# k computed by tokens in seven products of quarters, with its turns, banks and loads moved to match

## The chip, the cores and the metric

One core of one Trainium2 chip runs the kernel. The metric is the device time of one execution in microseconds (us). The kernel before took 1389.52 us, the median of three runs (1387.83 to 1391.02).

## The reference, cut to what matters

x has 4 sequences of 1024 tokens with 1024 channels. Every token is normalised, and two branches use it: an attention with a decaying state, and a gated ffn. All three weight matrices are rounded to -1, 0, 1 times one scale.

```python
x = L0_attn_x
xn = _layernorm(x, axis=-1)
s = _L0_attn_ref(xn, ...)
g = _silu(_L0_ffn_ref(xn, L0_ffn_weight, L0_ffn_bias))
x = x + s * g
```

Inside the attention (16 heads of 64, chunks of 128 tokens, a state S from chunk to chunk within a sequence):

```python
h = _rmsnorm(x, qkv_norm_w, eps)
qkv = h @ _weight_quant(qkv_w).T
scores = jnp.einsum('bhtd,bhsd,hts->bhts', qi, ki, mask)
intra = jnp.einsum('bhts,bhsd->bhtd', scores, vi)
cross = jnp.einsum('bhtd,ht,bhde->bhte', qi, lam_t, S)
o = scale * (intra + cross)
kv = jnp.einsum('bhtd,ht,bhte->bhde', ki, lam_rev, vi)
S = lam_T * S + kv
out = _rmsnorm(_rmsnorm(out, norm_w, 1e-06), proj_norm_w, eps) @ _weight_quant(proj_w).T
```

## The kernel before, in words

The 4096 tokens are handled as 16 blocks i of two chunks c of 128 tokens. Chunk number g = 2i + c; every eighth chunk ends a sequence, so blocks 3, 7, 11 and 15 hold a chunk that passes no state on. Everything is one program per engine with the order written out by hand, and semaphores between them (`s_...`). Activations are split into two 16-bit parts, high and low, each multiplied by fp8 weights, so every product is made twice and added in PSUM.

**Banks.** PSUM has four banks `ring`, used in the fixed order of the list `ring_uses`: use n may begin when use n-4 was emptied (`free_bank`, `emptied`). Four more banks, `att_ps`, hold scores, outputs and the state's update.

**A block on TensorE (PE), i from 2 on.** `project_qk(i, j)`, j = 0 to 7, makes q (j < 4) and k (j >= 4) by channels: 32 matmuls of 256 columns for each j. Between them stand, for the chunk before, `output_scale` (the sum of squares over channels, two tiny matmuls), `spread_gamma` (its inverse root, spread over partitions) and the two halves of `project_out`. Then v by tokens: where a full product of two chunks by 1024 channels takes eight products of quarters, v takes seven (p1 to p7, 8 matmuls of 512 columns each), with sums of quarters of the activations (`sum_b`, S1 to S4) and of the weights (`sum_v_weights`, T1 to T4) made on VectorE and GpSimd. ffn is made the same way (`sum_y`, `sum_weights`, `product`). Several products share a bank: `add_v`, `begin_v` and the `take_...` functions read it between two of them, so the later product waits for that reading. Then `attention(i, 0)` and `attention(i, 1)`: scores, k turned to tokens (`turn_k`, 8 transposes), outputs, state's update, `project_out` of chunk 0.

**VectorE (DVE).** At a block's start: statistics of block i+1 (`norm_stats`), sums of quarters and low parts (`sum_y`, `low_part`), `output_scale` (the small steps before the inverse root), `scale_o`, `split_o`, `sum_b`, `gate_out` of the chunk before, `low_b_sum`, then `centre` (two operations over 128x1024 for each chunk, which normalise x as turned by the host), then the second `gate_out`.

**ScalarE (ACT)** makes the high parts, empties q and k banks (`qk_out`) and applies silu. **GpSimd (POOL)** sums the squares (`sum_squares`), adds into the output (`add_out`), makes the inverse roots (`norm_scale`, `output_scale`), decays q and the state, and makes the sums of weights once, in block 1. **SyncE (SP)** issues all DMAs of the loop from one queue: store, mean and deviation of each token out to memory and back to all partitions (`spread_norm`), turned x (`load_turned`, which waits until block i's sums have been read out of `y` and `y_odd`), and x.

Of the kernel before, what the change touches and what calls it, by code (L numbers as in the profile page):

```python
# [36 lines left out]
def program(nc, x, qkv_w, proj_w, decay, ffn_w, ffn_b, norm_cols, x_turned, out):  # L37
# [17 lines left out]
    with ExitStack() as ctx:  # L55
# [49 lines left out]
        norm_rows = sb("norm_rows", [P, T, CHUNKS, 2])  # L105
# [6 lines left out]
        x_third = sb("x_third", [P, C])  # L112
        assert ARENA + SQ + C + C + C + C + CHUNKS * 2 * T + SUMS + CHUNKS * C == RAW * C
        gate_odd = sb("gate_odd", [P, CHUNKS, C])
        q_t = arena[:, Q_OFF:K_OFF].rearrange("p (r t) -> p r t", r=PR)
# [27 lines left out]
        ln = sb("ln", [P, 4, 24])  # L143
        og = sb("og", [P, 2, 4])
# [6 lines left out]
        norm_out = nc.dram_tensor("norm_out", [T, CHUNKS, 2], F32).ap()  # L151
# [34 lines left out]
        s_x = [sem(f"x_loaded{k}") for k in range(6)]  # L186
        s_out = [sem(f"out_stored{k}") for k in range(6)]
# [8 lines left out]
        s_vseed, s_vbase, s_vsum = sem("v_bank_begun"), sem("v_base_made"), sem("v_sum_made")  # L196
        s_zpart, s_zbase, s_zbias = sem("z_part_made"), sem("z_base_made"), sem("z_base_biased")
# [20 lines left out]
        def x_slot(i, c):  # L218
            if c == 1:
                return 2 + i % 3  # L220
            return i % 2 if i < 4 else (5, 0, 1)[(i - 4) % 3]

        def x_tile(i, c):
            k = x_slot(i, c)
            return xt[:, k, :] if k < 4 else x_third[:, :] if k == 4 else gate_odd[:, 0, :]

        def x_turn(i, c):

            return sum(x_slot(k, c) == x_slot(i, c) for k in range(i))
# [49 lines left out]
        def of_product(i, name):  # L279
            return 2 * CHUNKS * HALF + len(PRODUCTS) * (i - 2) + PRODUCTS.index(name) + 1  # L280

# [6 lines left out]
        def of_z(i, c, h):  # L288

            return of_ffn(i, c, h) if i < 2 else CHUNKS * HALF * i + ((0, 0), (1, 0), (1, 1), (0, 1)).index((c, h)) + 1  # L290
# [13 lines left out]
        def of_pair(i, c):  # L304
            return CHUNKS * (i - 2) + c + 1

# [20 lines left out]
        def v_weights_of(name):  # L327
# [5 lines left out]
            return qkv_q[:, k * CPH:(k + 1) * CPH, 2 * C + n * BANK:2 * C + (n + 1) * BANK]  # L333

# [85 lines left out]
        for i in range(NB):  # L420
# [13 lines left out]
            for c in range(CHUNKS):  # L434
                last = is_last(chunk(i, c))
# [8 lines left out]
                if not last:  # L444
                    ring_uses += [("k", i, c, 0), ("k", i, c, 1)]
# [5 lines left out]
                else:  # L451
# [4 lines left out]
                    for h in range(HALF):  # L456
                        ring_uses.append(("proj", i, 0, h))
                        if i == NB - 1:
                            ring_uses.append(("spread" if h else "total", NB - 1, 1))
        ring_uses += [("proj", NB - 1, 1, h) for h in range(HALF + 1)]  # L460
        ring_n = {use: n for n, use in enumerate(ring_uses)}

# [9 lines left out]
        def emptied(use):  # L472
# [8 lines left out]
            if kind == "ffn":  # L481
                return s_z, of_ffn(*use[1:])
            if kind == "v product":
# [7 lines left out]
            if kind == "v":  # L491
                return s_v, of_half(*use[1:])
            if kind == "k":
                return s_kl, HALF * passes_on(chunk(use[1], use[2])) + use[3] + 1
# [41 lines left out]
        def tensor_program(pe):  # L536
# [61 lines left out]
            def product(i, name):  # L598
# [8 lines left out]
                else:  # L607
# [3 lines left out]
                    if name == "p3":  # L611
                        pe.wait_ge(s_z, of_z(i, 1, 1))
                    else:
                        pe.wait_ge(s_zpart, of_zpart(i, ("p2", "p7", "p4").index(name)))
# [32 lines left out]

            def project_qk(i, j):
# [246 lines left out]
        def vector_program(dve):  # L895
# [381 lines left out]
            def attention(i, c):  # L1277
# [14 lines left out]
                if not last:  # L1292
                    decay_k(i, c)
# [799 lines left out]
```

## Time and profile before

| what | us |
|---|---|
| median of 3 runs | 1389.52 |
| the profiled execution | 1388.52 |
| its span, first to last instruction | 1386.8 |
| PE busy | 1344.0 |
| DVE busy | 950.2 |
| POOL busy | 603.6 |
| ACT busy | 552.1 |

The span is what the profile shows; 1.7 us of the execution lie around it. Matmuls are pipelined: one is shown for longer than the time from its start to the next one's start, so the cost of a row of them is read from starts. The granted TensorE clock is 0.995 on average over the span.

### The profile page before, as it was taken

The page shows a single profiled execution, that of the slowest core. Times are in us where ns is not written, and L with a number is a line of the kernel's source. Part 1 is how long each engine was busy: PE and PEld are TensorE (multiplying, and loading weights), DVE is VectorE, ACT ScalarE, POOL GpSimd, SP SyncE. Part 2 cuts the span into 40 slices and gives each one's busy share as a digit, 9 for nine tenths or more (in the row PEclk, how much of TensorE's full clock was granted, in tenths as well). Part 3 has the DMA queues.
Part 4 walks back from the last instruction along what each step waited for, and adds up shares of the span by engine and source line. Part 5 has one row for each costly group of instructions (what it writes and reads, how often), then busy time and mean ns, then how long its engine had stood idle before and what let it go on. Part 6 is the DMA issues. An engine that isn't in the chain of part 4 may idle for free.

```text
span 1386.8 us, 27408 instructions
## 1 busy us (share of the span) xinstructions
PE 1344.0 (97%) x11313; PEld 935.1 (67%) x11313; DVE 950.2 (69%) x1463; ACT 552.1 (40%) x1074; POOL 603.6 (44%) x528
## 2 busy tenths in 40 slices
PE   5999989899999999999999999999999999999998
PEld 2577667576676767767666676767767676776765
DVE  7895648486685857758576784858668585775835
ACT  5893224343343434334343423534334343433421
POOL 1533775263353525445351445426335352544332
PEclk9999989999999999999999999999999999999999
DMA  9521101103020020202002020110302002020000
GB/s 363 214 92 57 29 31 62 54 4 97 1 70 31 32 69 1 85 16 69 32 30 71 1 69 32 36 65 2 100 1 69 32 32 69 2 69 1 17 16 32
DMA packets 25534, 74.69 MB, mean 54 GB/s; under 512 B 6465, under 2 KB 6721, under 8 KB 25410
## 3 DMA queue, kind: packets, MB, share of 16 engines
q1 hardware_dynamic: 25120, 72.92, 15.5%
q8 instruction: 90, 1.47, 0.4%
q14 instruction: 34, 0.28, 0.1%
q10 hardware_dynamic: 290, 0.02, 0.0%
HBM read 56.12 MB, written 16.81 MB: 53 GB/s over the span
## 4 chain that ended last, share of the span: by engine, by line
PE 68%; POOL 14%; DVE 10%; issue 4%; ACT 2%; DMA 2%; SPq 0%; DVEq 0%; POOLq 0%; ACTq 0%
PE ring L658 20%; PE ring L617 12%; PE ring L643 12%; PE ring L777 8%; PE att_ps L693 4%; POOL sq L1855 4%; DVE b_lo L1097 4%; PE att_ps L739 2%; POOL xt L1876 2%; PE att_ps L735 2%; POOL sq L1851 2%; PE ring L701 2%; DVE o_lo L1243 1%; PE att_ps L716 1%; POOL diag L1870 1%
## 5 line engine op out<-in xcount | busy, mean ns | idle before, releaser
L658 PE MATMUL ring<-b_lo,qkv_q 128*128 128x256 f16 x2048 | 451.2, 273 | 0.0
L658 PE MATMUL ring<-b_hi,qkv_q 128*128 128x256 f16 x2048 | 451.2, 273 | 0.0
L658 PEld LDWEIGHTS ring<-b_hi,qkv_q 128*128 128x128 fp8e4 x2048 | 201.6, 98 | 27.8
L658 PEld LDWEIGHTS ring<-b_lo,qkv_q 128*128 128x128 fp8e4 x2048 | 200.3, 98 | 28.0
L777 PE MATMUL ring<-proj_q,o_hi 128*128 128x512 fp8e4 x496 | 188.1, 379 | 2.9 <-DVE o_lo L1243 2.9
L777 PE MATMUL ring<-proj_q,o_lo 128*128 128x512 fp8e4 x496 | 188.0, 379 | 0.0
L1599 ACT ACTIVATE arena<-ring,wscale 128x512 f32<-128x512 f32 x64 | 44.0, 687 | 213.0 <-PE ring L658 213.0
L1851 POOL TENSOR_TENSOR sq<-sq,cols 128x1024 f32<-128x1024 f32 x29 | 55.0, 1896 | 160.7 <-DVE b_lo L1097 152.3
L1876 POOL TENSOR_TENSOR xt<-xt,gate_even 128x512 f32<-128x512 f32 x40 | 59.9, 1507 | 147.4 <-DVE gate_even L1263 147.3
L1081 DVE SCALAR_TENSOR_TENSOR arena<-ring,wscale,arena 128x512 f32<-128x512 f32 x28 | 21.0, 750 | 139.2 <-PE ring L643 139.2
L1855 POOL TENSOR_TENSOR sq<-sq 128x1024 f32<-128x1024 f32 (+1 forms) x58 | 109.6, 1890 | 4.5
L1592 ACT ACTIVATE arena<-ring,wscale 128x512 f32<-128x512 f32 x64 | 43.9, 686 | 157.1 <-PE ring L658 157.1
L1128 DVE SCALAR_TENSOR_TENSOR gate_even<-ring,ln,gate_even 128x512 f32<-128x512 f32 x70 | 52.4, 749 | 68.5 <-PE ring L617 68.5
L739 PE MATMUL att_ps<-arena 128*64 128x128 f32 x1024 | 95.4, 274 | 0.0
L1811 POOL TENSOR_TENSOR gate_even<-gate_even,bias 128x512 f32<-128x512 f32 x14 | 17.7, 1264 | 167.1 <-ACT gate_even L1552 167.1
L735 PE MATMUL att_ps<-arena 128*64 128x128 f32 x896 | 89.1, 278 | 0.0
L777 PEld LDWEIGHTS ring<-proj_q,o_hi 128*128 128x128 f16 x496 | 48.6, 98 | 57.9 <-DVE o_lo L1243 4.0
L1181 DVE TENSOR_TENSOR arena<-att_ps,mask 128x512 f32<-128x512 f32 x128 | 79.5, 682 | 9.8 <-PE att_ps L693 9.8
L1826 POOL TENSOR_TENSOR arena<-arena,lam_q 128x512 f32<-128x512 f32 x56 | 71.3, 1285 | 32.4 <-PE att_ps L739 32.3
L777 PEld LDWEIGHTS ring<-proj_q,o_lo 128*128 128x128 f16 x496 | 48.6, 98 | 53.2
L1576 ACT ACTIVATE gate_even<-gate_even 128x512 f32<-128x512 f32 x60 | 37.3, 625 | 115.2 <-DVE gate_even L1128 115.2
L693 PEld LDWEIGHTS att_ps<-arena 64*128 64x128 f32 x1024 | 59.7, 188 | 17.7 <-issue 13.8
(222 smaller groups left out, 2864.0 us busy)
## 6 DMA issues: line engine op xcount, KB each, us to landing
raw<-in_qkv_w SPq DMA_DIRECT2D x24, 512.0 KB, 15.8
xt<-in_x SPq DMA_DIRECT2D x23, 512.0 KB, 3.5
out<-xt SPq DMA_DIRECT2D x22, 512.0 KB, 2.6
y<-in_x_turned SPq DMA_DIRECT2D x14, 512.0 KB, 6.1
y_odd<-in_x_turned SPq DMA_DIRECT2D x14, 512.0 KB, 6.8
raw<-in_ffn_w SPq DMA_DIRECT2D x8, 512.0 KB, 9.7
norm_rows<-norm_out SPq DMA_DIRECT2D x14, 256.0 KB, 5.2
raw<-in_proj_w SPq DMA_DIRECT2D x6, 512.0 KB, 4.5
```

The lines of the kernel that those rows point to most:

```text
L617: ins = pe.matmul(ring[:, b, :], of[:, j, :], weights_of(weights)[:, j, :], start=(begins and j == 0 and k == 0), stop=(j == CPH - 1 and k ...
L643: ins = pe.matmul(ring[:, b, :], of[:, j, :], v_weights_of(weights)[:, j, :], start=(name in ("p1", "p5") and j == 0 and k == 0), stop=(j ...
L658: ins = pe.matmul(ring[:, b, e * BT:(e + 1) * BT], qkv_q[:, cb, o:o + P], part[:, cb, :], start=(cb == 0 and part is b_hi), stop=(cb == NC ...
L693: ins = pe.matmul(att_ps[:, 2 * half + e, j, :], k_t[rows, r, ts], q_t[rows, r, ts], start=True, stop=True)
L735: pe.matmul(att_ps[e * D:(e + 1) * D, half, j, :], state[:, passes_on(g) % 2, r, e * D:(e + 1) * D], q_decay[:, r, :], start=True, stop=Fa ...
L739: ins = pe.matmul(att_ps[e * D:(e + 1) * D, half, j, :], v_tok[:, c, r * P + e * D:r * P + (e + 1) * D], scores_m[:, half, e, j, :], start ...
L777: ins = pe.matmul(ring[:, b, :], part[:, cb, :], proj_q[:, cb, cs], start=(cb == 0 and k == 0), stop=(cb == NCB - 1 and k == 1))
L1181: dve.tensor_tensor(scores_m[:, half, e, :, :], att_ps[:, 2 * half + e, :, :], mask[:, e, half * CPH:(half + 1) * CPH, :], ALU.mult).then_ ...
L1826: pool.tensor_tensor(q_decay[:, hs, :], q_t[:, hs, c * T:(c + 1) * T], lam_q[:, hs, :], ALU.mult).then_inc(s_ql, 1)
L1851: pool.tensor_tensor(sq[:, 1, :, :], sq[:, 0, :, :], over_tokens(cols[:, 1, :], T), ALU.mult).then_inc(s_sqw, 1)
L1855: pool.tensor_tensor(sq[:, :, 0:m, :], sq[:, :, 0:m, :], sq[:, :, m:2 * m, :], ALU.add).then_inc(s_sqw, 1)
L1876: pool.tensor_tensor(o, o, gate_of(i)[:, c, cs], ALU.add).then_inc(s_add, 1)
```

## The change

1. **k by tokens (from block 3, `BY_TOKENS`).** `project_qk` runs for j = 0 to 3 alone. `k_product` makes k as v is made: seven products, with the `sum_b` parts that v uses anyway, and sums of k's weights by `sum_k_weights` on POOL (T1 and T2 in block 2, T4 and T3 in block 3). The result is k by tokens (`k_tok`, in the memory of `gate_odd`); `turn_k` now turns it the other way, to channels, for every chunk, the last of a sequence too. ACT copies the turned k (`turned_k`); DVE decays k by tokens in place (`decay_k_tokens`) instead of from PSUM (`decay_k`).
2. **Orders from block 3 on** on PE, DVE and ACT are new: `attention_by_tokens`, and the block's start. On DVE the four `sum_b` now stand between the two `norm_stats`, ahead of `output_scale`, and `low_part` of the four sums after the first `gate_out`, right ahead of `centre(i + 1, 0)`.
3. **ffn's products** run p1, p6, p2, p5, p7, p3, p4 (before: p1, p6, p2, p7, p4, p5, p3).
4. **Totals and spreads** from chunk (2, 1) on stand in `att_ps` bank 3 (`aside`) instead of `ring`.
5. **x is loaded twice**: `load_x` into `xt[0:2]` for the statistics, `load_x_out` into `xt[2:4]` for the sum with the output. `norm_stats` of blocks 2 and 3 move to the start of blocks 1 and 2.
6. **`norm_rows`** has tokens innermost; the store of mean and deviation writes single fp32 elements.
7. **POOL in block 1**: `sum_v_weights` after `decay_state` and `decay_q`, not ahead of them.

```diff
-        norm_rows = sb("norm_rows", [P, T, CHUNKS, 2])
+        norm_rows = sb("norm_rows", [P, CHUNKS, 2, T])
...
+        BY_TOKENS = 3
+        PRODUCTS_LATER = ("p1", "p6", "p2", "p5", "p7", "p3", "p4")
...
+            def k_product(i, name):
+
+                if (i, name) == (BY_TOKENS, "p1"):
+                    pe.wait_ge(s_kwsum, 4)
...
+                elif name == "p4":
+                    pe.wait_ge(s_ksum, of_k_pair(i, 1))
...
+            def attention_by_tokens(i, c):
+                last = is_last(chunk(i, c))
+                scores(i, c)
+                if c == 0:
+                    v_product(i, "p4")
+                    product(i, "p1")
+                    product(i, "p6")
+                    turn_k(i, 1)
+                else:
+                    product(i, "p5")
+                    product(i, "p7")
+                    output_scale(i, 0)
+                    product(i, "p3")
+                    product(i, "p4")
+                    spread_gamma(i, 0)
+                outputs(i, c, 0)
+                outputs(i, c, 1)
+                if not last:
+                    update_state(i, c)
+                if c == 0:
+                    product(i, "p2")
...
+            for i in range(BY_TOKENS, NB):
+                project_qk(i, 0)
+                project_qk(i, 1)
+                output_scale(i - 1, 1)
+                project_qk(i, 2)
+                spread_gamma(i - 1, 1)
+                project_qk(i, 3)
+                k_product(i, "p1")
+                project_out(i - 1, 1, 0)
+                k_product(i, "p5")
+                k_product(i, "p2")
+                k_product(i, "p6")
+                project_out(i - 1, 1, 1)
+                k_product(i, "p3")
+                k_product(i, "p7")
+                k_product(i, "p4")
+                v_product(i, "p1")
...
+            def add_k(i, c):
+
+                dve.wait_ge(s_kps, of_k_product(i, "p7" if c else "p3"))
...
+                if more:
+                    norm_stats(i + 1, 0)
+                for name in Y_SUMS:
+                    sum_b(i, name)
+                if more:
+                    norm_stats(i + 1, 1)
+                output_scale(i - 1, 1)
...
+                gate_out(i - 1, 1, 0)
+                for name in Y_SUMS:
+                    low_part(i, name)
+                if more:
+                    centre(i + 1, 0)
+                gate_out(i - 1, 1, 1)
+                add_k(i, 0)
+                add_k(i, 1)
...
+                if i + 2 < NB:
+                    load_x(i + 2, 0)
+                    load_x(i + 2, 1)
+                if 2 < i + 1 < NB:
                     for c in range(CHUNKS):
                         load_turned(i + 1, c)
```

How the orders move, at three places. `ring` is the four shared banks, `arena` the memory of q, k, v, sums and state, `y` and `y_odd` the turned x of chunk 0 and 1.

PE in the changed kernel, block 5, from k's seventh product in program order to v's first (p7's last matmul, p4, v's p1):

```order
L731 MATMUL ring<-qkv_q,b_sum_lo 128x512
L731 MATMUL ring<-k_sum_last,b_hi 128x512 [waits k_sum_made]
L731 MATMUL ring<-k_sum_last,b_lo 128x512
...
L705 MATMUL ring<-qkv_q,b_hi 128x512 [waits k_tokens_made]
L705 MATMUL ring<-qkv_q,b_lo 128x512
```

Nothing stands between k's p7 and p4, and p4 waits for `k_sum_made`, DVE's `add_k(i, 1)`, which reads p7's bank. In the kernel before k had no such pair; v's p7 and p4 have a product of ffn between them (before) or the scores (now).

DVE at a block's start, before (block 10):

```order
L1263 SCALAR_TENSOR_TENSOR gate_even<-ring,wscale,gate_even 128x512 [waits gate_made,proj_ps] x2
L985 BN_STATS ln<-gate_odd 128x6 [waits x_loaded5]
...
L1044 TENSOR_TENSOR a_lo<-y_odd,a_hi 128x4x128 [waits a_hi_made]
L1060 TENSOR_TENSOR y_odd<-y_odd 128x512 [waits a_lo_made,b_weighed,b_lo_made]
L1060 TENSOR_TENSOR y_odd<-y,y_odd 128x512 [waits a_lo_made,y_summed]
L985 BN_STATS ln<-xt 128x6 [waits x_loaded3]
```

and in the changed kernel, from the same `gate_out` on:

```order
L1441 SCALAR_TENSOR_TENSOR gate_even<-ring,wscale,gate_even 128x512 [waits gate_made,proj_ps] x2
L1133 BN_STATS ln<-xt 128x6 [waits x_loaded0]
...
L1216 TENSOR_TENSOR arena<-arena 128x512 [waits b_summed,b_weighed] x4
L1133 BN_STATS ln<-xt 128x6 [waits x_loaded1]
...
L1428 TENSOR_SCALAR og<-att_ps 128x1 [waits sq_total_ps]
```

One low part and two sums of y stood between the statistics; now it is the four sums of b (`sum_b`), then the same second statistics and the small steps on `og`.

POOL in the changed kernel, at block 3's start, after the two norm scales:

```order
L2095 TENSOR_TENSOR ln<-ln,wscale 128x1 [waits ln_amp]
L2129 TENSOR_TENSOR k_sum_last<-qkv_q,k_sum 128x2048 [waits k_weights_summed]
L2129 TENSOR_TENSOR qkv_q<-qkv_q 128x4x512 [waits k_weights_summed,qk_ps]
L2202 TENSOR_TENSOR xt<-xt,gate_even 128x512 [waits gated,x_loaded_for_out1] x2
```

The two sums of k's weights (T4, T3) are new there; PE's first k product waits for both.

## Rows read from the trace of the kernel before

**Rows 1.** The page's part 1: busy us (share), instructions of each engine.
```profile
PE 1344.0 (97%) x11313; PEld 935.1 (67%) x11313; DVE 950.2 (69%) x1463; ACT 552.1 (40%) x1074; POOL 603.6 (44%) x528
```

**Rows 2.** Waits of PE: who waited for whom: us in total, times, longest us.
```profile
PE ring L643 <- ACT ring L1533: 3.8, 1, 3.8
PE att_ps L693 <- DVE arena L1216: 3.7, 1, 3.7
PE ring L670 <- DVE gate_even L1263: 2.9, 1, 2.9
```

**Rows 3.** Windows after two of these waits: busy by engine, PEclk, DMA share, GB/s.
```profile
174.60:178.00 3.40, 3.35 (x8) 1.19 (x9) 2.39 (x4) 0.00 (x0) 3.33 (x3) 0.51 0.36 147
257.10:262.00 4.90, 4.82 (x17) 1.95 (x18) 0.00 (x0) 1.31 (x3) 4.82 (x5) 0.72 0.40 127
```

**Rows 4.** Timeline of PE, block 8: first and last of 64 q matmuls, of 40 v matmuls.
```profile
714.92 0.27 PE L658 MATMUL ring<-b_hi,qkv_q 128*128 128x256 f16 x1
...
721.80 0.27 PE L658 MATMUL ring<-b_lo,qkv_q 128*128 128x256 f16 x1
...
750.68 0.38 PE L643 MATMUL ring<-qkv_q,b_hi 128*128 128x512 fp8e4 x1
...
759.10 0.38 PE L643 MATMUL ring<-qkv_q,b_sum_lo 128*128 128x512 fp8e4 x1
```

**Rows 5.** Timeline of PE, block 8: eight transposes of k, and what follows.
```profile
768.32 1.04 PE L701 MATMUL ring<-ident,arena 128*128 128x128 f32 x8
769.28 0.44 PE L739 MATMUL att_ps<-arena 128*64 128x128 f32 x4
```

**Rows 6.** Timelines of PE and DVE, block 7: a bank handed over and back.
```profile
700.36 0.38 PE L617 MATMUL ring<-ffn_sum,sum_lo 128*128 128x512 fp8e4 x1
...
701.67 0.38 PE L617 MATMUL ring<-ffn_q,sum_hi 128*128 128x512 fp8e4 x1 [0.60 <-DVE gate_even L1128]
```
```profile
700.77 0.75 DVE L1128 SCALAR_TENSOR_TENSOR gate_even<-ring,ln,gate_even 128x512 f32<-128x512 f32 x1 [0.98 <-PE ring L617]
```

**Rows 7.** Timeline of DVE, start of block 9, between and behind the statistics.
```profile
799.00 0.68 DVE L1044 TENSOR_TENSOR a_lo<-y_odd,a_hi 128x512 f16<-128x512 f32 x1
799.81 1.54 DVE L1060 TENSOR_TENSOR y_odd<-y_odd 128x512 f32<-128x512 f32 x1
801.38 1.10 DVE L1060 TENSOR_TENSOR y_odd<-y,y_odd 128x512 f32<-128x512 f32 x1
...
804.96 0.16 DVE L1252 SCALAR_TENSOR_TENSOR og<-og,ring 128x1 f32<-128x1 f32 x1
```

**Rows 8.** Timelines of POOL and PE, start of block 9.
```profile
801.90 2.94 POOL L1876 TENSOR_TENSOR xt<-xt,gate_even 128x512 f32<-128x512 f32 x2
805.20 0.94 POOL L1866 TENSOR_TENSOR og<-og,halves 128x1 f32<-128x1 f32 x1 [0.36 <-DVE og L1252]
```
```profile
807.35 0.49 PE L765 MATMUL ring<-diag,mean_sq 128*128 128x128 f32 x2 [0.42 <-POOL diag L1870]
```

**Rows 9.** Groups by line and form, DVE: busy us, mean ns of one | idle before.
```profile
L1068 DVE TENSOR_TENSOR arena<-arena 128x512 f32<-128x512 f32 x56 | 38.6, 690 | 4.7 <-DVE arena L1068 0.5
L1236 DVE TENSOR_TENSOR ow<-ow,ring 128x1024 f32<-128x1024 f32 x31 | 37.9, 1221 | 26.0 <-PE ring L765 25.9
```

**Rows 10.** The page's part 6, DMA issues: count, KB each, median us to landing.
```profile
xt<-in_x SPq DMA_DIRECT2D x23, 512.0 KB, 3.5
...
y<-in_x_turned SPq DMA_DIRECT2D x14, 512.0 KB, 6.1
```

**Rows 11.** Timelines of POOL and PE, block 8: squares summed, PE's total.
```profile
778.82 0.73 POOL L1860 TENSOR_TENSOR sq_sum<-sq 128x256 f32<-128x256 f32 x1
```
```profile
781.12 0.50 PE L757 MATMUL ring<-mean_w,sq_sum 128*128 128x1 f32 x4
```

**Rows 12.** POOL: a sum of weights (groups), block 3's last norm scale (timeline); PE, block 3's q.
```profile
L1804 POOL TENSOR_TENSOR v_sum_last<-qkv_q,v_sum 128x2048 fp8e4<-128x2048 fp8e4 x1 | 3.8, 3822 | 0.1
```
```profile
318.13 0.19 POOL L1782 TENSOR_TENSOR ln<-ln,wscale 128x1 f32<-128x1 f32 x1
```
```profile
302.04 0.27 PE L658 MATMUL ring<-b_hi,qkv_q 128*128 128x256 f16 x1
```

More of the change, by code:

```diff
@@ L216, in chunk, with x_new, x_out, mean_of @@
             return i * CHUNKS + c
[L218 to L229, printed above, removed]
+        def x_new(i, c):
+            if i == 0:
+                return xt[:, CHUNKS + c, :], (s_xo[c], DMA)
+            return xt[:, c, :], (s_x[c], DMA * i)
+        def x_out(c):
+            return xt[:, CHUNKS + c, :]
+        def mean_of(i, c, n=1):
+            return norm_pair[:, i % 2, c, 0:n]
+        def deviation_of(i, c):
+            return norm_pair[:, i % 2, c, 1:2]
         def gate_of(i):
@@ L419, in program @@
         ring_uses += [("v", 0, 0, 0), ("mean", PROJ), ("v", 0, 0, 1)]
-        for i in range(NB):
+        for i in range(BY_TOKENS):
             if i > 0:
@@ L745, in output_scale @@
             def output_scale(i, c):
-                b = free_bank("total", i, c)
+                if aside(i, c):
+                    pe.wait_ge(s_scm, 2 * HALF * (chunk(i, 1) + 1))
+                else:
+                    free_bank("total", i, c)
+                to = total_of(i, c)
                 if summed_at_once(chunk(i, c)):
@@ L763, in spread_gamma @@
                 pe.wait_ge(s_gamma, chunk(i, c) + 1)
-                b = bank_of("spread", i, c) if one_bank(i, c) else free_bank("spread", i, c)
-                pe.matmul(ring[:, b, 0:T], mean_sq[:, :], diag[:, c, :], start=True, stop=True).then_inc(s_spread, 1)
+                if aside(i, c):
+                    pe.wait_ge(s_os, chunk(i, c))
+                elif not one_bank(i, c):
+                    free_bank("spread", i, c)
+                pe.matmul(spread_of(i, c), mean_sq[:, :], diag[:, c, :], start=True, stop=True).then_inc(s_spread, 1)
             def project_out(i, c, half):
@@ L839, in attention @@
                     project_out(i, 0, 0)
-                    if not more:
-                        output_scale(i, 1)
                     project_out(i, 0, 1)
@@ L869, in tensor_program @@
             project_v(0, 0, 1)
-            for i in range(NB):
+            for i in range(BY_TOKENS):
                 if i > 0:
@@ L1011, in centre @@
                 to = y_turned[c]
-                rows = [norm_rows[:, :, c, k].unsqueeze(1).to_broadcast([P, NCB, T]) for k in range(2)]
+                rows = [norm_rows[:, c, k, :].unsqueeze(1).to_broadcast([P, NCB, T]) for k in range(2)]
                 dve.wait_ge(s_xt[c], DMA * n)
@@ L1247, in output_scale @@
                 k = og[:, c, :]
-                bank = ring[:, bank_of("total", i, c), :]
+                bank = total_of(i, c)
                 dve.wait_ge(s_sqt, g + 1)
@@ L1291, in attention @@
                     output_scale(i, 0)
-                if not last:
-                    decay_k(i, c)
+                decay_k(i, c)
                 if (i, c) == (0, 0):
@@ L1301, in attention @@
                         take_b(1, 1, 0)
-                    elif more:
+                    else:
                         split_b(i + 1, 0, 0)
@@ L1310, in attention @@
                 weight_o(i, c, 1)
-                if not last:
-                    add_state(i, c)
+                add_state(i, c)
                 if c == 0:
@@ L1323, in attention @@
                 else:
-                    if more and i > 0:
+                    if i > 0:
                         split_b(i + 1, 0, 1)
@@ L1398, in vector_program @@
                 round_weights(key)
-            for i in range(NB):
-                if 2 < i < NB - 1:
+            for i in range(BY_TOKENS):
+                if i > 0:
                     norm_stats(i + 1, 0)
@@ L1720, in scalar_program @@
                 weights_out(kind, t)
-            for i in range(NB):
+            for i in range(BY_TOKENS):
                 if i > 1:
@@ L2045, in sync_program @@
             for c in range(CHUNKS):
-                for i in range(NB - 3, NB):
-                    last = len(LAST_COLUMNS) - 1 if (i, c) == (NB - 1, 1) else 0
-                    sync.wait_ge(s_out[x_slot(i, c)], DMA * (x_turn(i, c) + 1 + last))
+                sync.wait_ge(s_out[c], DMA * (NB + c * (len(LAST_COLUMNS) - 1)))
         tensor_program(nc.tensor)
```

419 lines of the change are left out of this document (325 added, 94 removed).

## The prediction, written before the changed kernel was run

> **What bounds the kernel now.** I began with the page's busy times: PE is busy 1344.0 of 1386.8 us, DVE 950.2, POOL 603.6 [rows 1]. Nothing else is near, so only two things can move the time: work on PE, and waits of PE. The list of PE's waits came next. Its three longest behind the first 100 us are single ones, in blocks 1 and 2, of 3.8, 3.7 and 2.9 us [rows 2]; the rest come once in a block and are below 1 us. Third, the windows behind such waits: PE's granted clock is 0.51 over 3.4 us after one and 0.72 over 4.9 us after another [rows 3]. That is the lower level, 1.2 of 2.4 GHz, for some 3.3 and 2.7 us, so each of these waits costs about 1.5 us more than it shows. Last, I read PE's, DVE's and POOL's timelines of one block beside each other, since an order this tight has no slack that an average would show.
>
> A measurement of this kernel can tell about 0.2% (2.8 us) from no change; faster and slower mean more than that here.
>
> **The sum.** It is made against the profiled execution, 1388.5 us, which is 1.0 us under the median of the runs. 13 blocks (3 to 15) change; 12 of them (3 to 14) also prepare a next block.
>
> *k's products.* 64 q matmuls of 256 columns start 6.88 us apart, first to last: 6.88/63 = 0.109 us each. 40 of 512 columns take 8.42/39 = 0.216 each [rows 4]. k was 128 x 0.109 = 13.98 us and becomes 56 x 0.216 = 12.10: 1.88 less a block, **-24.5 us** in 13. All of it is on PE's path.
>
> *Turning.* k was turned for 28 chunks, and not for those that end a sequence; now for all 32. Eight transposes take 0.96 us [rows 5]: **+3.9** for four.
>
> *The new wait at k's p4.* p4 follows p7 on the same bank, and DVE's `add_k(i, 1)` must read between them. The kernel before had such a handover in ffn in the four blocks that end a sequence: the last matmul starts at 700.36, DVE reads from 700.77 for 0.75 us, PE goes on at 701.67 [rows 6]. That is 1.31 us where 0.216 would do: 1.1 us lost with nothing between. Thirteen times: **+14.2**. On PE all of v's products and both chunks of the block are queued behind it. It is 1.1 only if DVE is free. DVE's chain, from the end of `project_out(i-1, 1, 0)`, is `gate_out` 0.75, four low parts of 0.68 [rows 7], turned x of chunk 0, which SP may only issue then, `centre` (two operations that I take at 1.22, the price of a contiguous 128x1024 operation [rows 9]), `gate_out`, `add_k` twice, 0.75 each, and some 0.4 of handovers. With the load at 3.5 us, as x lands, this makes 12.0; with 6.1, as turned x lands behind other transfers [rows 10], 14.6. PE has 56 matmuls over the same time, 12.1, plus the 1.1 of the handover: 13.2. So 0 to 1.4 us come on top; two loads of x now stand ahead in SP's queue, which speaks for the late end, but were issued some us earlier. I take 0.4 in 12 blocks: **+4.8**.
>
> *The spread of the chunk before.* PE has waited for it: DVE's small steps end at 805.12, POOL starts 0.1 later, PE goes on at 807.35 [rows 7, 8]. In between is nothing but the chain, so whatever DVE has more ahead of the small steps goes through to PE. One low part and two sums of y leave (0.68, 1.54 and 1.10 [rows 7]), four sums of b come. Alone they take 0.69 each [rows 9]: by bare durations the difference is 2.76 - 2.06 = +0.7. But the sum of y that took 1.54 ran while POOL worked on squares, and POOL's two adds end only at 804.84 [rows 8]: at 1.5 each the four take 6.0, +2.7. I take 1.2, nearer the lower end, because of the three operations in that stretch one was not stretched at all: 12 x 1.2 = **+14.4**.
>
> *ffn's order.* With p7 now between p5 and p3, and p3 between p7 and p4, DVE has 1.7 us or more for each handover. The 0.77 that PE lost in four blocks (1.1 less 0.36 of the total's matmuls) goes: **-3.1**. But p7 left the stretch ahead of the total: PE reaches it 8 x 0.216 = 1.73 earlier, at 779.39 where it was 781.12, and POOL's squares end at 779.55 [rows 11]. That is 0.2 us of waiting in 13 blocks: **+2.6** (0 to 0.6 each).
>
> *Blocks 1 and 2.* Statistics earlier, POOL's sums of v's weights later, and a `gate_out` between the two `centre` take away what all three waits of [rows 2] hang on: 3.05 + 3.83 + 3.93 from start to start, and 1.5 us of low clock after each: **-15.4**. I saw no work that would take their place.
>
> *k's weights.* PE's first k product waits for four sums of weights. T1 and T2 fit into POOL's idle time of block 2. T4 and T3 stand behind the norm scales of block 3, which end at 318.32; two sums of 3.8 end at 326.0. Block 3 begins at 302.04 and PE reaches k after q (13.98), the total and the spread (0.7) and its wait (1.6), at 318.3 [rows 12]. **+7.7**, and 1.5 of low clock after such a wait: **+9.2** (7 to 12).
>
> *At nothing:* totals and spreads in `att_ps` (the bank's readers are done 1 us before); x twice (the loads are 3.5 us [rows 10] and not needed for tens of us); the store in single elements (turned x is later still); ACT's five more emptyings a block, 0.69 each (it is busy 40% of the time [rows 1]). If ACT were late, PE would wait for the k bank's seed at k's p2, where there is 0.1 us of room.
>
> Sum: -24.5 + 3.9 + 14.2 + 4.8 + 14.4 - 3.1 + 2.6 - 15.4 + 9.2 = **+6.1**: 1394.6 for the profiled execution, 1395.6 as a median. Its own range, with the ends of k's p4, the spread, the total and the weights that can come together, is 1382 to 1416.
>
> **The rule weighed.** The stretched sums of y [rows 7] show that DVE and POOL can hold each other up. The Trainium skill (SBUF — State Buffer, "SBUF: two separate sides") says more: a DVE instruction with two SBUF inputs and a POOL instruction exclude each other for the whole of an instruction. By that rule each of the four sums of b could wait out one POOL instruction, and the spread would cost the upper end. It is the third rival below.
>
> **The rivals.**
> 1. *The waits are covered: faster.* If DVE's start of the block is no slower than before, turned x lands in time and squares are ready, the terms of 4.8, 14.4 and 2.6 are nothing: 1388.5 - 15.7 = 1373, 1374 as a median. For it: DVE is idle 31% of the time [rows 1], and the terms that rest on PE's rows alone already sum to -15.7. Against it: DVE is on PE's path exactly at the two places where work is put in. It decides at 1.2 us in a block: if these three terms come to less than that in sum, the change is faster; more, slower.
> 2. *Low clock after the new waits: slower.* Waits of 3 to 4 us were followed by 1.2 GHz [rows 3], waits of 1.1 us [rows 6] were not. If the waits at k's p4 and at the spread, of 1 to 2.5 us each, are long enough in most blocks, 1.5 us come on top in 12: +18, 1414.
> 3. *DVE and POOL in turns: slower.* The spread at +2.7 in a block instead of 1.2: +18, 1414.
> 4. *Blocks 1 and 2 don't gain*, because another chain is right behind (the loads of x for block 2, POOL's ffn weights): +15, 1411.
>
> **How the numbers follow.** The sum as it stands 0.43, rival 1 0.30, rivals 2 and 3 0.11 each, rival 4 0.05. The predicted time is the likeliest case's, 1395.6. The range takes in rival 1 and the slow ones: 1372 to 1418. Faster by over 0.2%: rival 1, and 0.04 from the lower end of the likeliest: 0.34. Within 0.2%: 0.12, all from the likeliest. Slower: 0.54.
>
> **What would show it.** Right: blocks whose PE time without waits is 1.9 us shorter; a wait of PE in front of the last k weights product for DVE, 13 times, 0.9 us or more; a wait in front of the spread for POOL that grew from 0.4 to over 1 us; one wait of 7 us or more in block 3 for POOL's weights; none over 1.2 us in blocks 1 and 2. Wrong: DVE's small steps no later after a block's first q matmul than before, turned x landed before the low parts end, or a granted clock below 1.00 in the later blocks. If the longest waits of a block are for ACT, I looked at the wrong engine.

## The result: 8.9% slower, and the profile after

The changed kernel takes **1511.8 us** (median of 4 runs, 1509.0 to 1516.4); the kernel before, run beside it, 1388.8 (1387.8 to 1391.0). The ratio is 1.089, with a 95% interval of 1.085 to 1.092: 123 us more. My 1395.6 us was wrong, and so was the range up to 1418.

The page's head and part 1 of the changed kernel, the answer to [rows 1]:

```profile
span 1512.1 us, 25945 instructions
PE 1365.5 (90%) x10409; PEld 856.7 (57%) x10409; DVE 990.4 (66%) x1497; ACT 584.1 (39%) x1139; POOL 648.6 (43%) x532
```

PE was busy 97% of its span before and is busy 90% of it now, so the time went into waits. Its list of waits, which answers to [rows 2]:

```profile
PE ring L731 <- DVE gate_odd L1237: 39.8, 13, 5.0
PE ring L679 <- DVE gate_even L1284: 38.8, 13, 3.5
PE att_ps L867 <- POOL diag L2195: 23.9, 13, 2.1
...
PE ring L731 <- POOL qkv_q L2129: 7.9, 1, 7.9
PE ring L879 <- DVE o_lo L1421: 6.1, 6, 2.9
PE ring L867 <- POOL diag L2195: 5.9, 2, 5.2
```

The first line is k's p4 and `add_k` (predicted, at half of this). The second, ffn's p5 and `take_z11`, is not in my prediction at all. The third is the spread, the fourth k's weights, both as predicted; the last two hold two new waits in block 1. Measured from one matmul's start to the next, and less what the matmul itself takes, PE lost about 34 us in waits before and 142 now, 108 more; how the usual distance is set moves each sum by about 1 us.

The rest is the clock. The mean granted clock over the span was 0.995 and is 0.965. These windows lie around one wait at ffn's p5, in block 9 (window, its length, busy time of PE, PEld, DVE, ACT and POOL, then the granted clock, DMA share and GB/s):

```profile
934.10:937.10 3.00, 0.18 (x5) 0.03 (x1) 2.97 (x3) 0.12 (x1) 2.92 (x2) 0.98 0.00 0
937.10:940.10 3.00, 3.00 (x8) 1.05 (x9) 2.24 (x4) 0.52 (x1) 2.78 (x4) 0.50 0.00 0
940.10:943.10 3.00, 3.00 (x17) 1.61 (x16) 1.49 (x3) 0.00 (x0) 0.17 (x1) 0.95 0.00 0
```

PE stands still for 3 us, then starts 8 matmuls in the next 3 us where the window behind it has 17: it runs at 1.2 GHz, as behind the waits of [rows 3]. A mean clock of 0.965 over 1512 us is 53 us short of full speed, against 7 before.

Why PE waits at ffn's p5 is seen in DVE's and POOL's timelines of that place. DVE first:

```profile
930.51 1.40 DVE L1394 TENSOR_TENSOR arena<-arena,att_ps 64x512 f32<-64x512 f32 x2 [0.24 <-PE att_ps L810]
931.94 4.23 DVE L1359 TENSOR_TENSOR gate_odd<-gate_odd,lam_k 128x512 f32<-128x512 f32 x2
936.20 0.75 DVE L1284 SCALAR_TENSOR_TENSOR gate_even<-ring,ln,bias 128x512 f32<-128x512 f32 x1
```

and POOL, in the same microseconds:

```profile
930.98 1.90 POOL L2176 TENSOR_TENSOR sq<-sq,cols 128x1024 f32<-128x1024 f32 x1
932.95 4.34 POOL L2180 TENSOR_TENSOR sq<-sq 128x1024 f32<-128x1024 f32 x2
937.44 0.73 POOL L2185 TENSOR_TENSOR sq_sum<-sq 128x256 f32<-128x256 f32 x1
```

PE needs the bank of ffn's p1, which `take_z11` (936.20) empties. Ahead of it on DVE now stand the two operations of `decay_k_tokens(i, 1)`. They take 4.23 us together where the fastest one takes 0.68, and their neighbour ahead (930.51, two in 1.40 us), which reads PSUM, isn't stretched. Both inputs of `decay_k_tokens` are in SBUF; `decay_k`, which it replaces, read k from PSUM.

Last, the turned x of k's p4. SP's timeline in block 9:

```profile
880.31 0.38 SPq L2339 DMA_DIRECT2D norm_out<-norm_pair  x1
888.62 0.32 SPq L2342 DMA_DIRECT2D norm_rows<-norm_out  x1
888.98 0.91 SPq L2310 DMA_DIRECT2D xt<-in_x  x2
890.87 0.68 SPq L2328 DMA_DIRECT2D y<-in_x_turned  x1
```

and DVE's:

```profile
889.56 1.28 DVE L1192 TENSOR_TENSOR sum_lo<-y,sum_hi 128x512 f16<-128x512 f32 x2
898.49 1.23 DVE L1163 TENSOR_TENSOR y<-y,norm_rows 128x1024 f32<-128x1024 f32 x1 [7.65 <-DMA y<-in_x_turned]
```

SP stands 8 us behind the small store of the norms, then issues the rows of the norms, two loads of x and turned x within 2.3 us. Turned x isn't issued late: DVE's low parts, which it has to wait for, end at 890.84 (889.56 + 1.28). It lands late, 7.6 us after its issue, behind the loads issued just ahead of it, and DVE sits idle with `add_k` behind `centre`.

### The profile page after: what moved, and what is told of

Its sections match the earlier page's. It is cut to its first block, busy times and chain, and to the rows that moved or that the text cites. A ratio compares the mean times of both kernels' runs of the same rounds, so it can differ in the third digit from the quotient of the medians.

```text
span 1512.1 us, 25945 instructions
## 1 busy us (share of the span) xinstructions
PE 1365.5 (90%) x10409; PEld 856.7 (57%) x10409; DVE 990.4 (66%) x1497; ACT 584.1 (39%) x1139; POOL 648.6 (43%) x532
## 4 chain that ended last, share of the span: by engine, by line
PE 51%; DVE 16%; POOL 13%; issue 9%; DMA 8%; ACT 2%; SPq 1%; DVEq 0%; POOLq 0%; ACTq 0%
PE ring L705 11%; PE ring L679 11%; PE ring L746 6%; PE ring L731 5%; DMA y<-in_x_turned 5%; PE ring L879 5%; POOL sq L2180 4%; POOL xt L2202 3%; DVE b_lo L1253 3%; PE att_ps L783 2%; DMA norm_out<-norm_pair 2%; PE att_ps L833 2%; DVE arena L1394 2%; POOL sq L2176 2%; PE ring L795 2%
## 5 line engine op out<-in xcount | busy, mean ns | idle before, releaser
L746 PE MATMUL ring<-b_hi,qkv_q 128*128 128x256 f16 x1216 | 279.4, 279 | 0.0
L746 PE MATMUL ring<-b_lo,qkv_q 128*128 128x256 f16 x1216 | 279.3, 279 | 0.0
L2202 POOL TENSOR_TENSOR xt<-xt,gate_even 128x512 f32<-128x512 f32 x58 | 89.8, 1557 | 250.2 <-DVE gate_even L1441 250.1
L1359 DVE TENSOR_TENSOR gate_odd<-gate_odd,lam_k 128x512 f32<-128x512 f32 x52 | 73.9, 1460 | 95.2 <-PE ring L795 94.8
L746 PEld LDWEIGHTS ring<-b_hi,qkv_q 128*128 128x128 fp8e4 x1216 | 123.2, 101 | 18.4
L746 PEld LDWEIGHTS ring<-b_lo,qkv_q 128*128 128x128 fp8e4 x1216 | 121.9, 100 | 18.7
L1859 ACT ACTIVATE arena<-ring,wscale 128x512 f32<-128x512 f32 x64 | 43.9, 686 | 135.1 <-PE ring L746 135.1
L1441 DVE SCALAR_TENSOR_TENSOR gate_even<-ring,wscale,gate_even 128x512 f32<-128x512 f32 x58 | 43.4, 749 | 64.2 <-PE ring L879 63.8
L679 PE MATMUL ring<-ffn_sum,sum_hi 128*128 128x512 fp8e4 x112 | 49.0, 437 | 38.8 <-DVE gate_even L1284 38.8
L1804 ACT ACTIVATE gate_odd<-ring,wscale 128x512 f32<-128x512 f32 x26 | 17.9, 687 | 169.2 <-PE ring L731 169.2
```

Source lines behind the costliest of these rows:

```text
L679: ins = pe.matmul(ring[:, b, :], of[:, j, :], weights_of(weights)[:, j, :], start=(begins and j == 0 and k == 0), stop=(j == CPH - 1 and k ...
L746: ins = pe.matmul(ring[:, b, e * BT:(e + 1) * BT], qkv_q[:, cb, o:o + P], part[:, cb, :], start=(cb == 0 and part is b_hi), stop=(cb == NC ...
L2202: pool.tensor_tensor(o, o, gate_of(i)[:, c, cs], ALU.add).then_inc(s_add, 1)
```

## The experiments

Theory A, formed on this: the 108 us are waits that begin at two places of DVE's order, at the spread and at POOL's sums of weights, and the low clock behind the long ones makes them half as dear again. Theory B: DVE has no room in a block any more, and a wait taken away comes back elsewhere. All times below are medians of 4 runs; the kernel before, beside them, took 1389.4 to 1389.9.

**One edit at a time.** `take_z11` first:

```diff
-                    if not last:
-                        decay_k_tokens(i, 1)
                     take_z11(i)
+                    if not last:
+                        decay_k_tokens(i, 1)
```

> The changed kernel with one line moved: VectorE empties the bank of ffn's p1 (take_z11) before it weighs k of the second chunk (decay_k_tokens(i, 1)), not behind it. Theory A (a new handover on VectorE's queue): PE's wait in front of ffn's p5 (38.8 us in 13, 3.0 to 3.7 each from start to start, 41 in sum) goes, and with it about 1.5 us of low clock behind each, 19 in sum: 1512 - 60 = 1452 us. Rival B (VectorE is simply short of time in a block): the work moved stands ahead of the masking now, the wait comes back at the outputs or at k's p4, and the time stays above 1490 us.

Measured: 1504.4 us, only 7 less. The wait at p5 is gone, and PE's list has a new one:

```profile
PE ring L731 <- DVE gate_odd L1237: 42.2, 13, 5.9
PE att_ps L856 <- DVE arena L1350: 25.8, 13, 2.1
PE att_ps L867 <- POOL diag L2195: 23.8, 13, 2.1
```

The stretched operations now stand ahead of `mask_scores(i, 1)`, and PE may not write the total before that has read the bank (an order that the change itself made, with the total in `att_ps`). k's p4 and k's weights cost 4 us more between them. Rival B was right for this edit: the place was wrong, and work of 4 us fits into neither.

The turned x:

```diff
-                if more:
-                    centre(i + 1, 0)
                 gate_out(i - 1, 1, 1)
                 add_k(i, 0)
                 add_k(i, 1)
                 if more:
+                    centre(i + 1, 0)
                     centre(i + 1, 1)
```

> The changed kernel with centre(i+1, 0) behind gate_out(i-1, 1, 1), add_k(i, 0) and add_k(i, 1) on VectorE, so that nothing that the k bank needs stands behind the turned x. Theory A: PE's wait at k's p4 (41.9 us from start to start) falls to the bare handover, 1.1 x 13 = 14, and the low clock behind ten of the waits (1.5 each) goes too: 1512 - 28 - 15 = 1469 us. Rival B (the load is the bound and only moves): turned x still lands 8 us after VectorE has asked for it, centre holds up add_v, and PE waits at the fourth v product or at the scores instead: above 1490 us.

Measured: **1472.4 us**. The wait at k's p4 is 1.01 or 1.02 us each time, 13.2 in sum, where it was 41.9; the list, which leaves out part of each handover (the bank's way from PE to DVE and back), has it as

```profile
PE ring L731 <- DVE gate_odd L1237: 11.0, 13, 0.8
```

The clock's mean rises to 0.972. Theory A holds here in both numbers: of the 41.9 us, 13.2 are the handover and 28.7 are turned x, with the `centre` that waits for it.

The small steps of the chunk before:

```diff
+                output_scale(i - 1, 1)
                 if more:
                     norm_stats(i + 1, 1)
-                output_scale(i - 1, 1)
```

> The changed kernel with VectorE's small steps for the chunk before (output_scale(i-1, 1)) ahead of the second norm_stats. These are 1.8 us of work less in front of them. Theory A: PE's wait at the spread falls from 2.1 to about 0.4 us in 12 blocks, 20 us: 1492 us, with no change of the clock. Rival B: ScalarE's high parts or POOL's squares are as late, and less than 8 us come back: above 1504.

Measured: 1498.9 us, 13 less and not 20. The spread's wait is gone from block 3 on but for one of 0.95. But k's p4 costs 56.9 us instead of 41.9: PE comes to it 2 us sooner, turned x doesn't, and needs a median of 7.5 us from issue to landing where it took 6.3. The wait for k's weights grows in the same way, from 8.1 us to 9.9.

**What a wait costs.** The kernel before, with waits of set length and nothing else changed:

```diff
+                    if (c, half, cb) == (0, 1, CPH) and i in DELAYS:
+                        pe.wait_ge(s_reply, sum(n for j, n in DELAYS.items() if j <= i))
```

> The kernel before, plus waits of known length: in the middle of the last output product of the first chunk PE waits for a chain of small POOL operations (128x128) that it starts itself: 1 operation in blocks 3 to 5, 3 in blocks 6 to 8, 5 in blocks 9 and 10, 8 in blocks 11 to 13. At about 0.47 us an operation and 0.5 of handovers these are waits of 0.9, 1.9, 2.8 and 4.3 us, 27 in sum. Theory A (low clock only behind the long ones): granted clock 1.00 behind the first two groups, a stretch at 1.2 GHz worth some 1.5 us behind each of the five long ones: 1388.8 + 27 + 7.5 = 1423 us. Rival C (the clock has nothing to do with waits): 1416. Rival D (it falls behind each wait of 1 us or more): 1432.

Measured: 1422.5 us. The waits were 0.75, 1.7, 2.7 and 4.1 us from start to start, 25.0 in sum; 33 us were lost. Windows behind a wait of 2.68 (first line) and one of 4.11 (the other two):

```profile
975.00:978.00 3.00, 3.00 (x21) 1.92 (x22) 1.13 (x2) 0.00 (x0) 2.92 (x2) 1.00 0.00 0
1148.90:1151.90 3.00, 3.00 (x8) 1.07 (x9) 0.00 (x0) 0.00 (x0) 2.92 (x2) 0.50 0.00 0
1151.90:1154.90 3.00, 3.00 (x18) 2.09 (x17) 2.33 (x6) 0.00 (x0) 2.78 (x3) 0.62 0.00 0
```

Behind the eight shorter waits the clock was 1.00 throughout; behind the three of 4.1 it was 0.50 to 0.53 for 3 us and 0.62 to 0.91 for 3 more, which is 1.7 to 2.6 us each. So rivals C and D are out here: the clock makes a wait of 4.1 us about half as long again, and left those of up to 2.7 alone. In other kernels it didn't always do that (see the last section).

**The store of the norms.** In one piece a row, as before, and the rows read with a stride:

```diff
-                sync.dma_start(norm_out.rearrange("c k t -> t (c k)"), norm_pair[:, i % 2, :, :].rearrange("p c k -> p (c k)"),
-                               allow_slow_non_contiguous=True).then_inc(s_norm_out, DMA)
+                sync.dma_start(norm_out, norm_pair[:, i % 2, :, :]).then_inc(s_norm_out, DMA)
```

> The changed kernel with the norms stored as one piece a row and read with a stride by centre, as in the kernel before, and nothing else. SP waits for this store before it issues the loads of turned x. Theory A (the store in single elements is part of the late turned x): its landing falls from 7.2 us to about 4.2, the load of turned x is issued up to 3 us earlier, centre takes 2 x 0.8 longer, and PE's wait at k's p4 falls from 41.9 to about 25 us, with less low clock behind it: 1512 - 25 = 1487. Rival E (turned x waits for VectorE's low parts anyway): no change in the wait, centre's extra time comes on top, 1512 to 1530.

Measured: **1481.2 us**, 31 less. The issue-to-landing line of the store, changed kernel first, then this one:

```profile
DMA to landing us min/median/max: 4.1/7.2/10.6
```

```profile
DMA to landing us min/median/max: 1.4/3.3/5.6
```

SP's wait for it falls from 117.0 to 21.4 us in 14. SP's rows in block 9 of this kernel:

```profile
866.77 0.32 SPq L2341 DMA_DIRECT2D norm_rows<-norm_out  x1
867.13 0.91 SPq L2310 DMA_DIRECT2D xt<-in_x  x2
873.99 0.33 SPq L2328 DMA_DIRECT2D y<-in_x_turned  x1
```

Now the loads of x go out almost 7 us ahead of turned x. That one is issued no sooner, here too right behind the low parts (the first half of rival E holds, and my "up to 3 us earlier" doesn't). But it lands after a median of 3.6 us instead of 6.3, and k's p4 costs 25.4 us instead of 41.9. It isn't 13 because `centre` now reads with a stride: its two operations take 1.99 us each instead of 1.23. The wait did change, so rival E is out.

**DVE and POOL in turns.** Is it DVE's order, or POOL, that stretches `decay_k_tokens`? DVE's order stays as changed, and POOL gets one wait more:

```diff
                 if c == 1:
+                    if i >= BY_TOKENS:
+                        pool.wait_ge(s_kl, of_k_turn(i, 1, 1))
                     sum_squares(i, 0)
```

> The changed kernel, order of VectorE untouched, with one wait more on POOL: the squares of the first chunk (sum_squares(i, 0)) start only behind VectorE's decay_k_tokens(i, 1). Theory A (the missed wait in front of ffn's p5 is the two engines in turns, not the place in VectorE's queue as such): decay_k_tokens takes 1.3 us for its two operations, not 4.2, PE's wait at p5 falls from 3.0 to below 0.7, and the low clock behind it goes: 1512 - 33 - 25 = 1454 us, or up to 15 more if the later squares hold up the total. Rival F (the 4.2 us have another cause): decay_k_tokens stays at 4.2, the wait stays, and 1512 or more.

Measured: 1510.1 us. The group of `decay_k_tokens` (min, median and max in ns), changed kernel, then this one:

```profile
L1359 DVE TENSOR_TENSOR gate_odd<-gate_odd,lam_k x52: 682/1084/2829, 354.6 to 1476.9; 128x512 f32<-128x512 f32 x52
```

```profile
L1359 DVE TENSOR_TENSOR gate_odd<-gate_odd,lam_k x52: 681/689/693, 355.6 to 1473.1; 128x512 f32<-128x512 f32 x52
```

Not one of 52 is stretched, and PE's wait at p5 is gone (40.9 us from start to start). So the cause of the missed wait is shown: alone, the two operations would have fitted. The time isn't won all the same, because the squares are late for the total now:

```profile
PE att_ps L856 <- POOL sq_sum L2185: 28.1, 13, 2.2
```

That is 2.33 us in each of 13 blocks, with a granted clock below 0.8 in the 3 us behind ten of them, and k's p4 costs 46 us instead of 41.9. I had allowed up to 15 us for the later squares; together these took nearly all of the 58 that I expected.

The same in blocks 1 to 3, where POOL's sums of weights run for 3.8 us each:

```diff
-                        for name in ("T1", "T2", "T4", "T3"):
+                        sum_weights("T1")
+                        pool.wait_ge(s_olo, chunk(0, 1) + 1)
+                        for name in ("T2", "T4", "T3"):
                             sum_weights(name)
...
                     output_scale(i, 0)
                     if i == 1:
-                        sum_v_weights("T3")
+                        for name in ("T2", "T4", "T3"):
+                            sum_v_weights(name)
+                    if i == BY_TOKENS - 1:
+                        for name in ("T4", "T3"):
+                            sum_k_weights(name)
```

> The changed kernel with POOL's sums of weights moved in blocks 1 to 3: in block 1 POOL waits for split_o(0, 1) between T1 and T2 of ffn's weights; T2, T4 and T3 of v's weights come behind output_scale(1, 0); T4 and T3 of k's weights come in block 2 behind output_scale(2, 0). Theory A: the waits of 3.0 at 147 us, 5.3 at 200 and 7.7 at 325 go, 16 in sum, and the low clock behind them, about 2 each: 1512 - 22 = 1490 us. Test of VectorE and POOL in turns: VectorE's o_lo of 128x1024 took 4.60 us beside T2 where 1.23 is its price; if it waits for the whole POOL instruction it takes 1.23 now that T2 comes behind it; if 4.60 had another cause (its input came late, DMA traffic) it stays near 4.6.

Measured: 1519.7 us (1512.7 to 1523.1), if anything 8 *more*; the ranges of the two kernels overlap. The waits at 147, 200 and 325 us are gone, 16 us, and one half of the rest went as expected. In the changed kernel `split_o` took 4.60 us beside T2 (142.32) and 1.22 now that T2 follows it. DVE's row in the changed kernel, then here:

```profile
142.63 4.60 DVE L1421 TENSOR_TENSOR o_lo<-ow,o_hi 128x1024 f16<-128x1024 f32 x1 [3.87 <-ACT o_hi L1898]
```

```profile
143.94 1.22 DVE L1421 TENSOR_TENSOR o_lo<-ow,o_hi 128x1024 f16<-128x1024 f32 x1 [3.87 <-ACT o_hi L1898]
```

The other half ran into the same thing where I hadn't looked. DVE and POOL in block 1 of this kernel:

```profile
191.79 1.22 DVE L1414 TENSOR_TENSOR ow<-ow,ring 128x1024 f32<-128x1024 f32 x1 [1.53 <-PE ring L867]
192.93 9.16 DVE L1253 SCALAR_TENSOR_TENSOR b_lo<-y,cols,b_hi 128x128 f16<-128x128 f32 x4
202.01 1.21 DVE L1421 TENSOR_TENSOR o_lo<-ow,o_hi 128x1024 f16<-128x1024 f32 x1
```

```profile
190.11 3.84 POOL L2117 TENSOR_TENSOR v_sum<-qkv_q,v_sum 128x2048 fp8e4<-128x2048 fp8e4 x1
194.03 3.82 POOL L2117 TENSOR_TENSOR v_sum_last<-qkv_q,v_sum 128x2048 fp8e4<-128x2048 fp8e4 x1
198.00 3.95 POOL L2117 TENSOR_TENSOR qkv_q<-qkv_q 128x2048 fp8e4<-128x2048 fp8e4 x1
```

`scale_o` (191.79) reads PSUM and takes its 1.22 us beside a POOL sum. The four small operations of `split_b` behind it (1.14 us elsewhere in the trace) read only SBUF, take 9.16, and end 0.1 us after POOL's last sum. PE waited 8.9 us for `split_o`, and 4.3 in block 2. That takes 13 of the 16 us back. The others go at k's p4, which costs 52 us in this kernel instead of 41.9, 5.6 of them in block 3 where it was 1.0: PE comes to block 3 sooner, and turned x, whose load now follows more closely on those of x, takes 8.4 us to land there instead of 3.5.

The Trainium skill (SBUF — State Buffer, "SBUF: two separate sides") says that a DVE operation with two SBUF inputs and a POOL operation that reads SBUF share a pair of ports, and that the one that starts first holds it for its whole instruction while the other is blocked. The 0.69 against 2.83 us at `decay_k_tokens`, 1.22 against 4.60 at `split_o` and the unstretched `scale_o` agree with it.

**Together.** The edits of the second and third try, and `decay_k_tokens(i, 1)` behind `output_scale(i, 0)`, with neither a bank nor the masking behind it:

```diff
                 output_scale(i, 0)
+                if not last:
+                    decay_k_tokens(i, 1)
                 take_z12(i)
```

> The changed kernel with three edits on VectorE: centre(i+1, 0) behind add_k(i, 1), the small steps ahead of the second norm_stats, and decay_k_tokens(i, 1) behind output_scale(i, 0), so that neither the bank of ffn's p1 nor the masking stands behind it. Theory A: k's p4 costs 13 us in sum, the spread 1, ffn's p5 and the total nothing: 93 us of waits less, and the low clock behind some 23 waits of about 3 us and more goes, another 35 to 40 in sum: 1378 to 1388 us, about the kernel before. Rival B (VectorE is short of time and waits only move): in the single tries 16 and 13 us of the 41 and 24 freed were not kept, so something like 1400 to 1430, with a new longest wait in each block.

Measured: **1382.8 us**, 0.995 of the kernel before (0.994 to 0.997). Three moves on one engine give back 129 us; theory B is out as a whole. One of them is a little more than a move: in its old place `decay_k_tokens(i, 1)` ran in all 13 blocks, in its new one it is left out in the four that end a sequence (44 operations, not 52). Turned x comes no sooner here: it lands a median of 7.8 us after its issue, where it was 6.3. What changed is that nothing PE needs stands behind it.

With the sums of weights as in the kernel of 1519.7:

> All edits of the two kernels above together. Theory A: 1382 - 22 = 1360 us, 2% under the kernel before; the gains add, since they lie in different blocks and places. Rival B (waits move): over 1385.

Measured: 1378.1 us. Less than the 1360 hoped for, since 8.9 and 4.3 us in front of `split_o` came with it. So v's sums of weights went to where every DVE operation beside them reads PSUM, the first two of k's behind an `add_out` in block 2, and in block 2 `gate_out` went ahead of both `centre` (shown in part; these edits weren't tried apart):

```diff
                     add_out(i - 1, 1, 0)
+                    if i == BY_TOKENS - 1:
+                        for name in ("T1", "T2"):
+                            sum_k_weights(name)
...
+                    if i > 1:
+                        gate_out(i - 1, 1, 1)
                     centre(i + 1, 0)
```

> The kernel with all four edits, but POOL's sums of weights stand where VectorE has no operation with two SBUF inputs: T1, T2 and T4 of v's in block 1 ahead of the q decay of the second chunk, T3 ahead of output_scale; T1 and T2 of k's in block 2 behind the first add_out, T4 and T3 where T1 and T2 were. And in block 2 gate_out stands ahead of both centres. Theory A (a VectorE operation with two SBUF inputs waits for whole POOL instructions; the 8.9 and 4.3 us in front of the first output products of blocks 1 and 2 are that): these two waits and the one of 2.2 at 254 us go, 15 us, and some 6 of low clock behind them: 1378 - 21 = 1357 us. Rival B (those waits have another cause, or VectorE's sums are held up elsewhere in the same way): 1370 or more.

Measured: **1359.1 us**, with a mean clock of 1.000; the longest wait from 130 us on is 1.1. The place of k's sums isn't free of the same effect. Beside them DVE's four low parts of the sums of b, 2.49 us elsewhere, took

```profile
225.03 10.81 DVE L1221 TENSOR_TENSOR b_sum_lo<-arena,b_sum_hi 128x512 f16<-128x512 f32 x4
```

but PE had no wait there. Last, k's p4:

```diff
                 k_product(i, "p7")
-                k_product(i, "p4")
                 v_product(i, "p1")
+                k_product(i, "p4")
```

> The same with k's p4 behind v's p1 on PE (and ScalarE's seed of v's bank ahead of the last emptying of k's). Theory A: v's p1 (1.73 us) covers the handover to add_k and back, so the 1.0 us in front of k's p4 goes 13 times: 1357 - 13 = 1344 us, and PE's list of waits has nothing over 1 us behind block 3. Rival B: ScalarE's seed of v's bank or VectorE's add_k is then late for v's p2, and PE waits there instead: 1352 or more.

ACT's seed of v's bank moves ahead of the last emptying of k's with it. Measured: **1346.5 us**, 0.969 of the kernel before (0.967 to 0.970), and the fastest of all. Its page and its list of waits:

```profile
PE 1315.6 (98%) x10409; PEld 839.9 (62%) x10409; DVE 956.6 (71%) x1489; ACT 584.9 (43%) x1139; POOL 635.9 (47%) x532
```

```profile
PE ring L635 <- DVE y L1153: 12.7, 2, 11.9
PE ring L879 <- DVE o_lo L1421: 3.7, 8, 1.0
PE att_ps L609 <- DVE wtot L1058: 2.4, 1, 2.4
```

What is left over 1 us lies in the start of the kernel, but for one of 1.1 in block 1.

## Why the prediction was wrong, step by step

- **k's products (-24.5) and the turns (+3.9): right.** Take from each span PE's losses and what the clock is short of 1. Before: 1386.8 - 34 - 7 = 1346. The kernel of 1359.1 us: 1357.9 - 32 - 0 = 1326. That is about -20, where the two terms make -20.6.
- **The handover at k's p4 (+14.2): right.** 13.2 with nothing else in the way.
- **What comes on top there (+4.8): wrong, the first failed step.** It was 28.7. The chain that I added up was the right one, and turned x is issued when I said, right behind the low parts. The term that failed is its landing: I took 3.5 to 6.1 us, from loads of x that "were issued some us earlier", and put the store in single elements at nothing. But SP issues the loads of x only when that store has landed, in block 9 1.9 us ahead of turned x, and with them under way turned x took 5.9 to 8.3 us in blocks 4 to 13. PE's wait follows it one to one: 3.0 us where it took 6.1, 4.5 at 7.6, 5.2 at 8.3, and the bare 1.0 in blocks 3 and 14, where it took 3.5. (In block 13 its issue was 1.4 us late as well.) Giving the store its old form alone brought 31 us.
- **The spread (+14.4): the right mechanism, 5 us too small.** PE loses 2.03 us there in eight of the 12 blocks, 2.28 in three and 2.09 in block 3, 25.1 in sum, where it lost 5.6 before: 19.5 more. The four sums of b took 5.17 us in block 9, close to the stretched price of 6.0 that I had given to rival 3.
- **ffn's order (-3.1): right.** The four waits that I had at 0.77 (measured before: 0.74) are gone. The total (+2.6) didn't show, as PE came to it 3 us late; in the faster kernels it is 0.7 us three times.
- **Blocks 1 and 2 (-15.4): wrong.** The three waits went, and 3.0, 5.3 and 2.1 us came; the last is for ACT, and its cause wasn't looked for. "I saw no work that would take their place" was wrong twice: `split_o` now stood beside a sum of ffn's weights, and `output_scale(1, 0)` behind three sums of v's. Rival 4 had the outcome, with another cause.
- **k's weights (+9.2): right.** 8.1 us, and a window at 0.50 behind it.
- **The wait at ffn's p5 (not in the sum): 40.9 us, the largest failed step.** The sum has no term for `decay_k_tokens(i, 1)`, which took `decay_k`'s place on DVE and came to stand ahead of `take_z11`. Even its row in the order, at the price of an operation alone, would have shown nothing, as the kernel with POOL held back tells: it takes rival 3's mechanism, at a place that I didn't try it on. I had weighed the rule only where the diff added sums.
- **The clock: rival 2, and by far too small.** I gave it 18 us and a chance of 0.11, for waits of 1 to 2.5 us. Measured are 46 us (53 less 7). It can't simply be added to the waits: 108 + 46 - 20 is 134, and the spans differ by 125, since part of the low clock falls on time in which PE stood still.

Slower was the likelier side (0.54), but for 6 us, not 123: that it came is no credit to the sum. The mechanisms were nearly all on the page, but each was priced once and alone. Rivals 2, 3 and 4 all came true together, and they feed each other: a stretched operation makes a wait of 3 us, and behind most of these the clock is at its lower level.

## What to carry to other kernels

When a queue is full, list for each moved or new operation who stands *behind* it, on DMA queues too, and which transfers it pushes together: here the form of a 2 KB store cost 31 us. Check each new DVE operation with two SBUF inputs against what POOL does in the same microseconds, and price it with POOL's instruction added. And give long waits a price beyond their length: the set ones of 4.1 us cost 1.7 to 2.6 us more, and from 2 us on many waits here were followed by the lower clock.

The change was worth keeping: its order was what was wrong. Three edits on DVE made 1511.8 into 1382.8, and the rest 1346.5.

## What the runs showed of the hardware

- **The clock behind waits.** I looked at the 3 us behind each wait of 0.6 us or more, from 130 us on, in 13 traces. Behind 190 waits below 1.6 us the granted clock never fell. Behind 197 of 1.6 to 3.6 us it was below 0.9 in 107; behind 77 longer ones in 74. The shortest wait with such a fall behind it was 1.65 us. Of 107 waits of 2.0 to 2.5 us, 64 had one, yet the two set ones of 2.7 had none. In the middle group the same wait at the same place goes either way: of the ten waits of 2.98 or 2.99 us at ffn's p5 in the changed kernel, eight were followed by 0.50 to 0.67 and two by 1.00. What decides it there stays open.
- **A moved bottleneck can cost twice.** With POOL held back, the waits summed to 135 us instead of 142, and the time stayed within 2 us of the changed kernel's.
- **A landing time depends on the neighbours.** The same load of turned x took a median of 6.3 us or 3.6 us from issue to landing, with only a 2 KB store in another form. The changed kernel itself tells the form from the bunch. In block 14 the store is in single elements as everywhere, but there is no x left to load ahead of turned x:

```profile
1350.26 0.32 SPq L2342 DMA_DIRECT2D norm_rows<-norm_out  x1
1354.12 0.33 SPq L2328 DMA_DIRECT2D y<-in_x_turned  x1
```

It landed 3.5 us after its issue, as in block 3, where the loads of x went out 13 us ahead. So the bunch is what makes it slow; this is read from the traces, and no edit tried it alone. Why the store in single elements takes 7.2 us where the other takes 3.3, no run shows.

Not tried: the kernel before with only its blocks 1 and 2 put in order. By the first point on why the prediction was wrong, the change itself is worth about 20 us of the 43 between 1389.9 and 1346.5; the rest is waits and low clock that the kernel before had too.
